# A fused adaLN block on one core: order of the first loads, the first attention group's load, and where two small tables are made

## The reference

```
mod = (silu(c) @ wmod).reshape(8, 6, 1, 256)     # shift, scale, gate, shift, scale, gate
ga, gb = guarded gates: sign(g) * max(|g|, 0.25)
h = layernorm(x) * (1 + ca) + sa
x = x + ga * attention(h)          # 16 heads of 16; keys and values through a latent of 64;
                                   # rotary by head index; full softmax over 1024 tokens
h = layernorm(x) * (1 + cb) + sb
x = x + gb * ffn_stack(h)          # 2 layers: windowed attention (8 heads of 64, window 128, each head's
                                   # q and k l2-normalized, scaled by q_scale / k_scale, rotated by xpos
                                   # tables), then layernorm, 256 -> 2 x 682, gelu gate, -> 256
```

## Time and profile before

| | us |
|---|---|
| median of 3 runs (4456.62 to 4467.39) | 4466.62 |
| the profiled execution | 4465.89 |
| its span, first to last instruction | 4464.1 |

### The profile page before, as it was taken

The page is one execution under the profiler, slowest core; times in us unless marked ns, Lnnn a source line. Parts: engine busy times, 40 slices in busy tenths (PEclk is TensorE's granted clock), DMA queues, the critical chain, the costliest instruction groups (busy, mean ns, idle before and its releaser), DMA issues. The chain is left out here.

```text
span 4464.1 us, 79549 instructions
## 1 busy us (share of the span) xinstructions
PE 4130.9 (93%) x26918; PEld 2629.4 (59%) x26918; DVE 3555.6 (80%) x7972; ACT 2784.3 (62%) x6236; POOL 1568.3 (35%) x2441
## 2 busy tenths in 40 slices
PE   6679999999999986499999998999899999998998
PEld 3323333333333324377777776888777777777887
DVE  6589999999999957788888886656688888885665
ACT  3438888888888871167766665444567666663343
POOL 0000001000000003456655554454456555554555
PEclk9979999999999987799999999999999999998999
DMA  6833343233332306510000100221010010101321
GB/s 223 283 55 55 50 77 57 41 57 46 52 53 44 57 7 210 163 44 26 25 26 27 39 24 19 86 60 55 20 48 25 25 28 25 39 17 57 88 72 56
DMA packets 366416, 274.97 MB, mean 62 GB/s; under 512 B 98921, under 2 KB 333241, under 8 KB 366017
## 3 DMA queue, kind: packets, MB, share of 16 engines
q1 hardware_dynamic: 364608, 269.02, 24.7%
q10 hardware_dynamic: 1408, 0.93, 0.1%
HBM read 165.98 MB, written 102.81 MB: 60 GB/s over the span
## 5 line engine op out<-in xcount | busy, mean ns | idle before, releaser
L881 ACT ACTIVATE fa_P<-fa_pS 128x512 f32<-128x512 f32 x2048 | 1111.7, 595 | 324.9 <-PE fa_pS L805 276.1
L908 DVE TENSOR_REDUCE fa_mx<-fa_pR 128x2 f32<-128x1024 f32 x1024 | 1205.3, 1220 | 92.0 <-PE fa_pR L786 77.6
L1668 POOL TENSOR_TENSOR wa_pn<-wa_pr,wa_ri 128x512 f32<-128x512 f32 (+1 forms) x512 | 673.1, 1316 | 495.4 <-DVE wa_ri L1720 495.1
L1606 ACT ACTIVATE wa_pr<-wa_sm,wa_mn 128x256 f32<-128x256 f32 (+1 forms) x1024 | 496.7, 488 | 177.8 <-DVE wa_mn L1711 151.5
L822 PE MATMUL fa_pO<-fa_P,fa_V 128*32 128x512 f32 x4096 | 555.6, 615 | 0.0
L805 PE MATMUL fa_pS<-fa_Q,fa_K 50*128 50x512 f32 x2048 | 512.0, 497 | 41.9 <-ACT fa_P L881 11.2
L805 PEld LDWEIGHTS fa_pS<-fa_Q,fa_K 50*128 50x128 f32 x2048 | 192.6, 185 | 526.5 <-ACT fa_P L881 439.7
L786 PE MATMUL fa_pR<-fa_K,fa_Q 48*128 48x512 f32 x2048 | 429.5, 463 | 55.2 <-DMA fa_K<-parts_d 36.2
L753 POOL COPY fa_V<-fa_Vc 128x512 f32<-128x512 f32 x32 | 19.6, 613 | 1243.8 <-DMA fa_Vc<-v_d 1243.8
L1457 PE MATMUL wa_pQK<-wa_wqkv,wa_xT 128*128 128x512 f32 x1536 | 423.6, 412 | 6.3 <-DVE wa_qa L1757 6.3
L1711 DVE CUSTOM_DVE_ANT_0 wa_sm<-wa_pS,wa_mask 128x256 f32<-128x256 f32 (+1 forms) x1024 | 356.9, 402 | 21.2 <-issue 16.4
(11 more groups left out here) (185 smaller groups left out, 7062.8 us busy)
## 6 DMA issues: line engine op xcount, KB each, us to landing
parts_d<-pj_parts SPq DMA_DIRECT2D x64, 512.0 KB, 4.1
fa_Q<-parts_d SPq DMA_DIRECT2D x192, 128.0 KB, 4.2
fa_K<-parts_d SPq DMA_DIRECT2D x192, 128.0 KB, 7.2
pj_x<-in_L_attn_x SPq DMA_DIRECT2D x16, 512.0 KB, 6.2
v_d<-pj_v SPq DMA_DIRECT2D x16, 512.0 KB, 6.0
fa_Vc<-v_d SPq DMA_DIRECT2D x32, 256.0 KB, 8.4
fa_Q<-fa_nrow SPq DMA_DIRECT2D x512, 2.0 KB
att_d<-fa_att SPq DMA_DIRECT2D x64, 128.0 KB, 2.2
```

Of the source, the lines that this page charges most:

```text
L881: nc.scalar.activation(Pr[:, k % 2, h, :], pS[:, (s * exped.per + u) % T, :], ACT.Exp).then_inc(exped.sem, 1)
L908: nc.vector.tensor_reduce(mx[:, q // QB, :, a, q % QB, kh], row_slot(), AX.X, ALU.max).then_inc(row_free, 1)
L1606: last = nc.scalar.activation(pr[:, hp % 2, hh, lo:], sm[:, hp % 2, hh, lo:], ACT.Exp, bias=mn[:, p, h:h + 1], scale=-1.0, accum_out=rs[:, ...
L1668: nc.gpsimd.tensor_tensor(pn[:, hp % 2, :, lo:], pr[:, hp % 2, :, lo:], inv, ALU.mult).then_inc(s["weighted"].sem, 1)
```

## The change

What it does:

- *First loads.* SyncE loads the identity, x of chunk 0, the two up-projection weights, the query weight, then x of chunks 1 to 3, then the modulation rows' weights. ScalarE's queue loads c, the down-projections, the rope table, the modulation columns' weights (before: on SyncE's), then wo. One semaphore becomes four (`low_in`, `wq_in`, `wo_in`, `cols_in`). The rotary table and the scales are no longer loaded here. The zero rows are stored before the loop.
- *The loop.* VectorE does all statistics and the normalization of chunk n+2 before both `low`s of chunk n. ScalarE copies the first half of the values between the q cast and the k cast. The three side jobs are gone from the loop.
- *Group 0* has buffers of its own from the start (`FirstGroup`: `fg_q`, `fg_k`, `fg_v`); POOL sets its rows of ones in the projections, and SyncE loads it after chunk 3's stores (`GROUP_AT`). At the end of the projections SyncE waits for this load, and no longer for the last stores; SyncE and POOL wait for those in full attention (`settle`), POOL sets the ones of the other two key buffers, and SyncE loads group 1 after that.
- *Modulation rows* are made by TensorE in full attention's prologue, after the ninth row-score tile, into `fa_pS`; ScalarE copies them out, and VectorE's `guard` stands at step 4 of the last group.
- *Rotary tables*: `load_weights` loads the fixed table and six pieces of the scales (ten transfers instead of four), and POOL multiplies them after the last split piece (`scale_trig`), in group 15 of full attention and in chunk 10 of the first feed-forward. TensorE and VectorE of the window block wait for it. The DRAM copy of the scaled tables is gone.

The core of the diff (full attention's indexing of separate buffers and the signatures left out):

```diff
...
+class FirstGroup:
+        self.q, self.k = sb("q", [P, GH // 2, N], F32R), sb("k", [P, GH // 2, N], F32R)
+        self.v = sb("v", [P, N // P, GH * HD])
...
+    def settle(self, eng):
+        for p in range(2):
+            eng.wait_ge(self.stored.sems[p], self.stored.upto(NC - 2 + p))
+        eng.wait_ge(self.prepared, 16 * 2 * DEPTH)
...
                 for n in range(NC):
                     store(n, n % 2)
                     if n + R < NC:
                         load(n + R)
-                    if n == PREPARED_AT:
...
-                sp.wait_ge(prepared, 16 * (len(hi_d) + 2))
-                sp.wait_ge(stored.sems[0], stored.upto(NC - 2))
-                sp.wait_ge(stored.sems[1], stored.upto(NC - 1))
+                    if n == GROUP_AT:
+                        for p in range(2):
+                            sp.wait_ge(stored.sems[p], stored.upto(p))
+                        sp.wait_ge(fg.ones, 2)
+                        load_stacks(sp, parts_d, fg.q, fg.k, 0, 0, fg.stack_in)
+                        load_values(sp, v_d, fg.v[:], 0, 0, fg.v_in)
+                sp.wait_ge(fg.stack_in, 16 * 12)
+                sp.wait_ge(fg.v_in, 16)
...
                 for n in range(NC):
-                    following = n + 2 < NC
-                    if following:
-                        stats_of(n + 2, (n + 2) % R, range(0, 6))
+                    if n + 2 < NC:
+                        stats_of(n + 2, (n + 2) % R, range(LN_INCS))
+                        normalize(n + 2, (n + 2) % R)
                     low(n, n % 2, 0)
-                    if following:
-                        stats_of(n + 2, (n + 2) % R, range(6, 10))
                     low(n, n % 2, 1)
-                    if following:
-                        stats_of(n + 2, (n + 2) % R, range(10, LN_INCS))
-                        normalize(n + 2, (n + 2) % R)
-                    if n in TRIG_AT:
-                        scale_trig(TRIG_AT.index(n))
-                    if n == GUARD_AT:
-                        guard()
...
+                    v_out(0)
+                    act.wait_ge(k_done.sem, k_done.upto(n))
+                    nc.scalar.copy(parts[:, p, 1, 0], pK[:]).then_inc(hi_ready.sem, 1)
+                    v_out(1)
...
-                sp.wait_ge(ones, NB)
-                load(0, 0)
+                fg.settle(sp)
+                sp.wait_ge(ones, 2 * (NB - 1))
                 load(1, 1)
                 max_rows(0, 0, 0)
...
                 drive(sp, body)
+                sp.wait_ge(guarded, 1)
+                sp.dma_start(mod_d[:, 2:6, :], mods[:]).then_inc(rows_kept, 16)
                 store(GROUPS - 1, 1)
...
                 nc.gpsimd.memset(V[:, :, :, :, HD:2 * HD], 1.0).then_inc(v_ones, 1)
+                pool.wait_ge(v_ones, 1)
+                fg.settle(pool)
+                for s in range(1, NB):
+                    for e in range(2):
+                        nc.gpsimd.memset(Ks[s][e * TOP + 32:e * TOP + 64].bitcast(F32), 1.0).then_inc(ones, 1)
+                        pool.wait_ge(ones, 2 * (s - 1) + e + 1)
...
                 for j in range(ROWS // 2):
                     row_scores(0, 0, j)
+                    if j == ROWS // 4:
+                        mod_rows()
...
+                pe.wait_ge(rows_out, 2)
                 drive(pe, body)
...
+                        if k == 4 and is_last(n):
+                            guard()
...
+    def scale_trig(self, pool, layer):
+
+        pool.wait_ge(self.w_low[layer], self.PIECES)
+        self.nc.gpsimd.tensor_tensor(self.trig[:].rearrange("p w a c -> p w (a c)"), self.trig_in[:],
+                                     self.scales[:].unsqueeze(1).to_broadcast([P, NW, 4 * DH]),
+                                     ALU.mult).then_inc(self.w_low[layer], 1)
...
```

More of the change, by code:

```diff
@@ L451, in turn @@
                     last.then_inc(turned.sem, 1)
-                def mod_rows():
-                    pe.wait_ge(rows_in, 16)
-                    pe.wait_ge(v_ready.sem, v_ready.upto(ROWS_AT))
-                    for bank in range(2):
-                        for k in range(KT):
-                            last = nc.tensor.matmul(pL[0:B, bank, :], cT[:, k, :],
-                                                    wmod[:, k, (bank + 1) * 512:(bank + 2) * 512],
-                                                    start=(k == 0), stop=(k == KT - 1))
-                        last.then_inc(tensor_made, 1)
                 def body(n, p):
@@ L559, in body, with v_out @@
                     nc.scalar.copy(parts[:, p, 0, 0], pQ[:]).then_inc(hi_ready.sem, 1)
-                    act.wait_ge(k_done.sem, k_done.upto(n))
-                    nc.scalar.copy(parts[:, p, 1, 0], pK[:]).then_inc(hi_ready.sem, 1)
-                    for bank in range(2):
+                    def v_out(bank):
                         j = 1 - bank
@@ L632, in full_attention @@
         att = sb("fa_att", [P, 2, QB, GH * HD])
+        mods = sb("fa_mods", [B, 4, D])
+        ga, gs = sb("fa_guard_a", [B, 2, D]), sb("fa_guard_s", [B, 2, D])
+        V = sb("fa_V", [P, NB, KB, GH, 2 * HD])
+        Pr = sb("fa_P", [P, 2, GH, HALF])
+        OT = sb("fa_OT", [P, 2, HALF])
+        wh.stage(ctx, 0)
+        Qs = [fg.q] + [sb(f"fa_Q{s}", [P, PAIRS, N], F32R) for s in range(1, NB)]
+        Ks = [fg.k] + [sb(f"fa_K{s}", [P, PAIRS, N], F32R) for s in range(1, NB)]
+        Vc = [fg.v] + [sb(f"fa_Vc{s}", [P, KB, GH * HD]) for s in range(1, NB)]
         pS = ctx.enter_context(nc.psum_tensor("fa_pS", [P, T, HALF], F32))
@@ L692, in load @@
                     b, g = n // NG, n % NG
[L693 removed]
+                    if n >= NB:
                         sp.wait_ge(scored.sem, scored.upto(n - NB))
[L695 to L702 removed]
+                    load_stacks(sp, parts_d, Qs[s], Ks[s], b, g, stack_in.sems[s])
                     if n >= NB:
                         sp.wait_ge(v_spread.sem, v_spread.upto(n - NB))
[L705 to L706 removed]
+                    load_values(sp, v_d, Vc[s][:], b, g, v_in.sems[s])
                 def max_rows(n, s, half):
@@ L832, in turn_sums, with mod_rows @@
                     last.then_inc(row_full, 1)
+                def mod_rows():
+                    pe.wait_ge(fg.rows_in, 16)
+                    for bank in range(2):
+                        for k in range(KT):
+                            last = nc.tensor.matmul(pS[0:B, bank, :], w.cT[:, k, :],
+                                                    w.wmod[:, k, bank * HALF:(bank + 1) * HALF],
+                                                    start=(k == 0), stop=(k == KT - 1))
+                        last.then_inc(rows_done, 1)
                 for j in range(ROWS // 2):
                     row_scores(0, 0, j)
+                    if j == ROWS // 4:
+                        mod_rows()
                 turn_max(0, 0)
@@ L886, in body @@
                             copy_out(n, 0)
+                for bank in range(2):
+                    act.wait_ge(rows_done, bank + 1)
+                    nc.scalar.copy(mods[:, 2 * bank:2 * bank + 2, :],
+                                   pS[0:B, bank, :].rearrange("p (r c) -> p r c", r=2)).then_inc(rows_out, 1)
                 drive(act, body)
@@ L893, in _ @@
                 use = [0, 0]
-                for s in range(NB):
-                    for e in range(2):
-                        last = nc.vector.memset(Ks[e * TOP + 32:e * TOP + 64, s].bitcast(F32), 1.0)
-                    last.then_inc(ones, 1)
                 def row_slot():
@@ L2022, in body @@
                         wh.low(pool, layer + 1, n - SPLIT_AT)
+                    if not final and n == SPLIT_AT + wh.PIECES:
+                        pool.wait_ge(s["u_split"].sem, s["u_split"].upto(g(n)))
+                        wh.scale_trig(pool, layer + 1)
                 drive(body)
```

229 lines of the change are left out of this document (111 added, 118 removed).

## The result

The changed kernel took 4399.74 us (median of 4 runs, 4392.85 to 4406.78), the kernel before 4467.01 us beside it: ratio 0.9865, 95% interval 0.9851 to 0.988. Forecast were 4407 us, 4391 to 4424. The profiled run took 4404.63 us (span 4402.6), 61.3 less than the 4465.89 of before; the forecast, made against that run, was 59.2 less.

What follows compares the result with a forecast made beforehand. The prediction took the transfer queue, 347 GB/s, to bound the changed projection loop. Loop with start -33.9, border -29.7 and modulation rows +4.4 gave -59.2 us: 4407 us forecast, own range 4399 to 4417, with rivals 4391 to 4424.

Steps and rivals of the forecast that it cites:

- The start: First loads: with split semaphores and wo last, chunk 0 starts 5.9 us earlier, at 20.4 us.
- Both TensorE waits go, chunk 1 at 34.9: Projection loop: waits of 1.67 and 0.61 us vanish; chunk 1 starts at 34.9, TensorE's floor is 8.40 a chunk.
- The queue's 347 GB/s make 9.07 a chunk: Projection loop: 3.15 MB a chunk at 347 GB/s take 9.07 us, so transfers set the pace.
- the prediction's own sign: Projection loop: chunk starts 9.0 to 9.2 us apart from chunk 4 on, one interval near 14 after the group load.
- The group load, 1.8 MB, costs 5.2: Projection loop: the first group's 1.8 MB of stacks and values cost about 5 us, counted in the loop's bytes.
- The border, 29.7: Projections to full attention: the gap between matmuls is 6.5 us in place of 36.2, 29.7 gained.
- The modulation rows, 4.4: Full attention's prologue: TensorE's 5.3 us for the rows, partly covered by VectorE's waiting tiles, lose 4.4 us.
- Costed at nothing: Guard in the last group, POOL's table multiplication (5.2 us) and six more small loads: taken as covered, no cost.
- The sum: Whole kernel: -33.9 (loop with start) - 29.7 (border) + 4.4 (modulation rows) = -59.2 us.
- The queue keeps up: Rival, projection loop: the queue gives 380 GB/s, TensorE bounds, last matmul ends at 162; 4397 us, chance 0.19.
- The border did not stay dear: Rival, into full attention: group 1, maxima's rows or instruction loading come late; 4424 us, chance 0.16.
- The clock rival: Rival: TensorE enters full attention at 1.2 GHz and stays there; kernel slower, some 4485 us, chance 0.03.

Runs made afterwards that it cites:

- old_start: Changed kernel, but TensorE turns no weight before the query weight and wo have landed, and wo loads ahead of the modulation columns: 4399.06 us, ratio 0.9882.
- early_load: Changed kernel with the x load of chunk n+4 issued ahead of chunk n's stores, same bytes and four buffers: 4385.25 us, ratio 0.9848.
- no_preload: Changed kernel with group 0's stacks and values loaded in full attention behind the last stores, as before: 4410.84 us, ratio 0.9891.
- after_again: The changed kernel run once more, unedited: 4409.97 us (median of 6), ratio 0.9889.
- best: Changed kernel with eight x buffers, earlier x loads, group loads spread, modulation rows after the last projection matmul, two unread matmuls a step in the last group: 4373.36 us.
- filler: Changed kernel with four unread matmuls a step added in full attention's last group: 4393.33 us, ratio 0.9859.
- old_loop: Changed kernel with the projection loop's earlier orders on ScalarE (value copies) and VectorE (statistics) put back: 4431.3 us, ratio 0.9942.

## Why the prediction was right, point by point

- **The start.** 5.95 gained, 5.9 forecast. The cause was half wrong: old_start, without TensorE's finer waits, loses only 0.5 to 0.7 us, so nearly all of it came from the new order of the loads.
- **Both TensorE waits go, chunk 1 at 34.9.** 34.83. The floor is 8.15 and not 8.40: the 8.40 was read over a chunk in which a wait cut up the transposes, which is probably the difference.
- **The queue's 347 GB/s make 9.07 a chunk.** This step failed, though its sum held. By the prediction's own sign the intervals were to be 9.0 to 9.2 from chunk 4 on; they were not. It took the rate in proportion to the share (319 at 0.92, so 347 at 1), and 346 GB/s is what the loop asked for, not what the queue gives: it gives 380 to 412. The bound was the loop that the prediction had worked out one sentence earlier and set aside at 8.35: statistics, normalization, subtractions, stores, and the x load behind them. With this trace's 7.0 us to landing in place of 6.2 it comes to 5.40 + 2.45 + 2.64 + 7.0 = 17.5 for two chunks, 8.7 each; the last six intervals average 8.80. early_load is the proof: same bytes, L 9.3 us less.
- **The group load, 1.8 MB, costs 5.2.** It cost 14.99 + 12.01 - 2 x 8.15 = 10.7, since its 128 KB pieces pass at 172 to 255 GB/s; with the x load moved (early_load) 7.4, with six buffers 6.3, so some 3 to 4 of the 10.7 are again the late x. A rate that was too low for the stores and one that was too high for the stacks cancelled: 171.5 forecast, 171.49 measured. That was luck. early_load shows the first error, the slices the second.
- **The border, 29.7.** 30.1 measured; no_preload shows 17.9 of it to be the preload. The forecast took 4.9 to the end of SyncE's last issue and 1.6 from there to the first matmul; measured were 177.02 - 171.49 = 5.53 and 0.55. The 1.6 leaned on a release of POOL at 214.31, which in the earlier trace rows is a length of idle time and not a moment; the last store's landing at 214.28 happens to stand beside it. The order of what is late next held to a microsecond.
- **The modulation rows, 4.4.** 4.9. TensorE took 5.86 for them, with 0.50 granted from 178 to 190 us.
- **Costed at nothing.** POOL's table multiplication took 4.6 us (5.2 forecast). In the feed-forward, its cover did not quite do. POOL itself was not late; VectorE's subtraction ran beside it and took 4.95 us, where 23 of the 32 of this kind take 1.23 and eight 1.68, and TensorE's next chunk waits 0.97 us for it:

```profile
2965.61 4.61 POOL L1219 TENSOR_TENSOR wa_trig<-wa_trig_in,wa_scales 128x2048 f32<-128x2048 f32 x1
2966.35 4.95 DVE L2001 TENSOR_TENSOR ff_hT<-ff_hF,ff_hT 128x1024 fp32r<-128x1024 f32 x1 [3.50 <-ACT ff_hT L2140]
...
2971.35 1.67 PE L2099 MATMUL ff_pG<-ff_hT,ff_w 128*128 128x512 f32 x6 [0.97 <-DVE ff_hT L2001]
```

- **The sum.** -33.9 - 30.1 + 4.9 and -0.9 between the first and the last scores make -60.0 at full attention's end (its last matmuls start at 1621.33 in place of 1681.31). The other 1.5 of the span came later, and no run here took them apart. The fair comparison is that of the two traces, 61.3 against 59.2, as both have the slow last group; two of the changed kernel's four runs lie 10 us lower, which brings its median 7 below the forecast.
- **The rivals.** "The queue keeps up" had the truth about the queue (0.19), but not its consequence, since the x load and not TensorE was next; with the load moved (early_load) its last projection matmul came where this rival had it, 162.98 against 162. The border did not stay dear. The clock rival did not come: the prologue ran at 0.50, and 1.00 was back some 13 us after the first scores (0.50 from 219 to 232 us, 1.00 from 234). TensorE did fall back to 0.50 while at work, but in the last group and not in the first, and it does so in the kernel before as well.

## What to carry to other kernels

A transfer share near 1 is not a bound until the same mixture has been seen at no higher rate: look at the slices, and set the rate asked for (bytes over the interval) beside them. Where a load into a ring of buffers stands behind the stores of its own step, count the loop that this closes; moving the issue costs nothing and gave here 9.3 us, where two more buffers gave 10.5. When a kernel's times stand in two clusters, look for a stretch in which one engine has less to do than elsewhere, and compare traces of either kind there before any edit is judged by its median.

## What the runs showed of the hardware

- TensorE's granted clock fell to 0.50 inside a block in which it was still busy for 7.3 of 10 us, in some executions and not in others (after_again from 1570 to 1590, with the fall behind it, old_start from 1567), and stayed at 1.00 with 8.2 to 8.5 (best) and 9.1 to 9.2 (filler):

```profile
1579.70:1589.70 10.00, 7.27 (x48) 2.00 (x40) 0.00 (x0) 8.32 (x16) 0.00 (x0) 0.98 0.00 0
1589.70:1599.70 10.00, 8.63 (x34) 1.74 (x32) 0.00 (x0) 6.01 (x11) 0.00 (x0) 0.50 0.00 0
```

```profile
1577.10:1587.10 10.00, 7.28 (x48) 1.93 (x46) 0.02 (x1) 8.26 (x17) 0.00 (x0) 1.00 0.00 0
1587.10:1597.10 10.00, 7.84 (x52) 2.40 (x52) 0.68 (x2) 8.34 (x16) 0.00 (x0) 1.00 0.07 16
```

The first pair is after_again, the second old_start: the same work at the same busy share, once with the fall and once without.

- Transfers of 128 KB onto 16 partitions pass at 148 to 255 GB/s where those of 512 KB over 128 partitions pass at 380 to 416, both at a share of 0.9 or more. They differ in size and in partitions, and no run tells these apart.
- One VectorE instruction of 128x1024 took 4.95 us while POOL multiplied 128x2048 for 4.61 us beside it, and 1.23 us in most other places (changed kernel, 2966).
- The latent copy of chunk 1 came at 33.7 to 37.7 us in kernels with the same start. The loads are the smaller part: TensorE's first turn, which waits for them, came at 9.26 to 10.50. The same 16 small matmuls took 3.42 us in five of these traces (copy at 35.6 to 37.7) and 1.85 to 2.13 in the others (33.7 to 35.1; old_start, which turns at 10.89, 34.5; old_loop, with the old order, 36.3).
